# A third score bank in place of the maxima's start ring, one value product per slot, maxima spread between the scores, and the chunk loop written out

## The reference

```python
x = x + cross_attention(layernorm(x), ctx, ctx, tau, delta)      # 16 heads of 16, softmax over 1601
x = x + top1_expert_ffn(layernorm(x))                            # 8 experts, all computed, the chosen one kept
x = x + windowed_attention(ctx, layernorm(x), len, p_t)          # window of 256 keys, tanh
x = x + slot_ffn(layernorm(x))                                   # 64 slots, top-8 routing, slots gathered over all tokens
```

## Time and profile before

| | us |
|---|---|
| three timed runs, median | 1281.99 (1279.39 to 1282.0) |
| the profiled execution, its own time | 1280.34 |
| its span, first to last instruction | 1278.7 |
| PE busy | 1095.6 |
| VectorE (DVE) busy | 828.6 |
| ScalarE (ACT) busy | 549.9 |
| mean granted clock | 0.887 |

### The profile page before, as it was taken

The page is one execution under the profiler, slowest core; times in us unless marked ns, Lnnn a source line. Parts: engine busy times, 40 slices in busy tenths (PEclk is TensorE's granted clock), DMA queues, the critical chain, the costliest instruction groups (busy, mean ns, idle before and its releaser), DMA issues.

```text
span 1278.7 us, 20158 instructions
## 1 busy us (share of the span) xinstructions
PE 1095.6 (86%) x6460; PEld 438.7 (34%) x6460; DVE 828.6 (65%) x1814; ACT 549.9 (43%) x1020; POOL 44.2 (3%) x54
## 2 busy tenths in 40 slices
PE   6357999999999998898999989889999888977556
PEld 3232233333433333333333334323333243344324
DVE  4447988888776766676667765667667657644232
ACT  4121266666644444555444454555444436500220
POOL 3200000000000000000000000000000000010000
PEclk9876699999999987998999888989999889978765
DMA  8995000000000000001000000010000000100321
GB/s 240 144 114 184 1 8 7 14 14 2 30 14 1 13 1 1 14 2 48 2 13 1 14 1 13 1 49 1 14 1 14 1 14 1 46 1 0 109 75 66
DMA packets 44281, 41.19 MB, mean 32 GB/s; under 512 B 10109, under 2 KB 42334, under 8 KB 43914
## 3 DMA queue, kind: packets, MB, share of 16 engines
q1 hardware_dynamic: 41594, 38.17, 12.8%
q10 hardware_dynamic: 2496, 1.35, 0.7%
q0 software_dynamic: 80, 0.26, 0.2%
HBM read 29.52 MB, written 10.59 MB: 31 GB/s over the span
## 4 chain that ended last, share of the span: by engine, by line
PE 58%; DVE 16%; issue 13%; DMA 5%; SPq 4%; DVEq 2%; ACT 1%; POOL 0%; POOLq 0%; ACTq 0%
PE ps_o L748 17%; PE ps_m L672 15%; PE ps_e L903 11%; DVE mx L1055 10%; PE ps_m L779 7%; DMA k_stack<-q_stack 1%; DMA k_parts<-attn_chunk 1%; PE ps_m L969 1%; SPq L376 1%; PE ps_m L839 1%; PE ps_m L858 1%; PE ps_m L799 1%; SPq L352 1%; DMA q_stack<-mrow 1%; PE ps_m L860 1%
## 5 line engine op out<-in xcount | busy, mean ns | idle before, releaser
L1055 DVE TENSOR_REDUCE mx<-ps_m 128x1 f32<-128x401 f32 x1102 | 585.9, 570 | 259.6 <-PE ps_m L672 256.8
L564 ACT ACTIVATE probs<-ps_e 128x512 f32<-128x512 f32 (+1 forms) x832 | 457.7, 596 | 497.8 <-PE ps_e L903 496.5
L672 PE MATMUL ps_m<-k_stack,q_stack 99*128 99x401 bf16 x1102 | 401.5, 367 | 60.4 <-DVE mx L1055 51.7
L903 PE MATMUL ps_e<-q_stack,k_stack 101*128 101x512 bf16 (+1 forms) x832 | 337.3, 405 | 8.4 <-issue 7.0
L748 PE MATMUL ps_o<-probs,v_heads 128*32 128x256 f32 (+1 forms) x3328 | 280.3, 410 | 0.0
L672 PEld LDWEIGHTS ps_m<-k_stack,q_stack 99*128 99x128 bf16 x1102 | 109.4, 99 | 309.2 <-DVE mx L1055 266.5
L903 PEld LDWEIGHTS ps_e<-q_stack,k_stack 101*128 101x128 bf16 (+1 forms) x832 | 84.6, 102 | 152.8 <-ACT probs L564 64.8
L779 PE MATMUL ps_m<-expert_w,xnT 128*128 128x512 f32 x256 | 121.3, 605 | 6.3 <-DVE xb L1119 4.7
L748 PEld LDWEIGHTS ps_o<-probs,v_heads 128*32 128x32 f32 (+1 forms) x3328 | 67.1, 110 | 156.9 <-issue 132.5
L1119 DVE SCALAR_TENSOR_TENSOR xb<-ps_m,hot,xb 128x256 f32<-128x256 f32 x112 | 54.2, 484 | 17.9 <-PE ps_m L779 8.3
L779 PEld LDWEIGHTS ps_m<-expert_w,xnT 128*128 128x128 f32 x256 | 47.1, 194 | 47.9 <-issue 35.8
(11 more groups left out here) (213 smaller groups left out, 612.5 us busy)
## 6 DMA issues: line engine op xcount, KB each, us to landing
q_stack<-q_parts SPq DMA_DIRECT2D x114, 64.0 KB, 2.2
k_stack<-k_parts SPq DMA_DIRECT2D x18, 256.0 KB, 14.0
q_parts<-attn_chunk SPq DMA_DIRECT2D x6, 384.0 KB, 5.5
expert_w<-in_expert_wT SPq DMA_DIRECT2D x2, 1024.0 KB, 5.9
xres<-in_x SPq DMA_DIRECT2D x4, 512.0 KB, 3.5
x<-xres SPq DMA_DIRECT2D x4, 512.0 KB, 3.8
probs<-x SPq DMA_DIRECT2D x1, 2048.0 KB, 10.7
out<-probs SPq DMA_DIRECT2D x4, 512.0 KB, 2.9
```

The lines of the kernel that those rows point to most:

```text
L564: act.activation(probs[0:n, k % 2, h, :], ps_e[h % 2][0:n, :], ACT.Exp).then_inc(s["exp_done"], 1)
L672: pe.matmul(ps_m[:, u % 2 if banks == 2 else (UNITS * n1 + u) % banks, 0:SPLIT], qst[0:MAX_ROW, g, h, P * t:P * t + P], kst[0:MAX_ROW, HG ...
L903: pe.matmul(ps_e[h % 2][0:n, :], kst[0:ROWS, HG * g + h, P * st:P * st + n], qst[0:ROWS, g, h, :], start=True, stop=True).then_inc(s["qk_r ...
L1055: dve.tensor_reduce(mx[:, q, col:col + 1], ps_m[:, bank_of, 0:SPLIT], AX.X, ALU.max)\
```

## The change

- `ps_e` gets a third bank; a score waits for the exp three scores back instead of two.
- `ps_x` is no longer a bank of its own but the last bank of `ps_m`; turned maxima ("m") and turned `ps_o` ("o") become jobs that take their turn with the jobs of `behind` in two banks. Since they come at other places than once per chunk, jobs are numbered over all chunks.
- The ring of the maxima has two banks everywhere, at the start too.
- The value product is one per head and slot, over 512 tokens, at the slot's end.
- A unit follows each score; the fifth stands ahead of score 2, or, in a slot with an expert, a unit stands between the two halves of the expert's contraction and one behind each of the other scores. No unit follows the value product.
- VectorE takes unit 0 before its step of `behind` and does `max_columns` right behind the last unit of a group.
- The loops over chunks are Python loops, so offsets and waits are constants.

The rest of the diff is the new argument of `bank`, `filled` and `taken`, and constants in place of `bass.ds`.

```diff
+RING = 2
+EB = 3
...
-JOBS = (["ota", "otb", "y0", "y1", "t1a", "t1b", "router"] + [f"e{i}" for i in range(4)] + ["gateT"] + [f"e{i}" for i in range(4, 8)]
-        + ["gb0", "gb1"] + [f"e{i}" for i in range(8, 16)]
-        + ["t2a", "t2b", "score0", "score1", "aTa", "aTb", "z0", "z1", "t3a", "t3b", "h", "logits", "slots", "alphaT"])
-JOB = {name: i for i, name in enumerate(JOBS)}
-USES = len(JOBS) // 2
-assert len(JOBS) % 2 == 0
+BEHIND = {3: ["ota", "otb"], 5: ["y0"], 6: ["y1"], 9: ["t1a", "t1b"], 10: ["router"],
+          **{11 + i: [f"e{i}"] for i in range(8)}, 15: ["gateT", "e4"], 19: ["gb0", "gb1"],
+          **{20 + i: [f"e{8 + i}"] for i in range(8)}, 30: ["t2a", "t2b"], 31: ["score0", "score1"], 34: ["aTa", "aTb"],
+          35: ["z0"], 36: ["z1"], 39: ["t3a", "t3b"], 40: ["h"], 41: ["logits"], 44: ["slots", "alphaT"]}
...
+def has_expert(k):
+
+    return 11 <= k < 19 or 20 <= k < 28
...
+def job_numbers():
+
+    order = [("m", 0)]
+    for c in range(NC):
+        for k in range(SLOTS):
+            g, st = divmod(k, ST)
+            if c:
+                order += [(name, c - 1) for name in BEHIND.get(k - SHIFT, [])]
+            if st == 2 and (c or g):
+                order.append(("o", NG * c + g - 1))
+            if max_end(k - 1) is not None:
+                order.append(("m", NG * c + max_end(k - 1)))
+    order.append(("o", NG * NC - 1))
+    order += [(name, NC - 1) for k in range(SLOTS) for name in BEHIND.get(k, [])]
+    return {job: i for i, job in enumerate(order)}
+
+
+JOB = job_numbers()
...
-        ps_e = [ps(f"ps_e{i}", [P, CT]) for i in range(2)]
-        ps_m = ps("ps_m", [P, 4, CT])
+        ps_e = [ps(f"ps_e{i}", [P, CT]) for i in range(EB)]
+        ps_m = ps("ps_m", [P, RING + 2, CT])
         ps_o = ps("ps_o", [P, CT])
-        ps_x = ps("ps_x", [P, CT])
+        ps_x = ps_m[:, RING + 1, :]
...
-        def bank(job):
-            return ps_m[:, 2 + JOB[job] % 2, :]
+        def bank(job, c):
+            return ps_m[:, RING + JOB[job, c] % 2, :]
 
         def bank_free(eng, job, c):
 
-            need(eng, bank_taken[JOB[job] % 2], USES * c + JOB[job] // 2)
-
-        def filled(mm, job):
-            mm.then_inc(bank_filled[JOB[job] % 2], 1)
+            need(eng, bank_taken[JOB[job, c] % 2], JOB[job, c] // 2)
...
-                    act.activation(probs[0:n, k % 2, h, :], ps_e[h % 2][0:n, :], ACT.Exp).then_inc(s["exp_done"], 1)
+                    act.activation(probs[0:n, k % 2, h, :], ps_e[(HG * (SLOTS * c + k) + h) % EB][0:n, :], ACT.Exp).then_inc(s["exp_done"], 1)
...
             def take_o(c, g):
                 act.wait_ge(s["pv_done"], SLOTS * c + ST * (g + 1))
-                need(act, s["att_ready"], NG * c + g)
+                if NG * c + g:
+                    wait_filled(act, "o", NG * c + g - 1)
...
-            def max_unit(u, c, j, banks=2):
+            def max_unit(u, c, j):
 
 
                 g, n1 = j % NG, NG * c + j
                 t, h, q = u // (QUARTERS * HG), (u // QUARTERS) % HG, u % QUARTERS
                 if u == 0:
                     pe.wait_ge(q_loaded[j % NG], 96 * (c + j // NG + 1))
-                need(pe, s["max_taken"], UNITS * n1 + u + 1 - banks)
-                pe.matmul(ps_m[:, u % 2 if banks == 2 else (UNITS * n1 + u) % banks, 0:SPLIT], qst[0:MAX_ROW, g, h, P * t:P * t + P],
+                need(pe, s["max_taken"], UNITS * n1 + u + 1 - RING)
...
             def max_rows(n1):
 
-                need(pe, s["att_ready"], n1 - 1)
                 pe.wait_ge(s["mx_ready"], n1 + 1)
-                pe.transpose(ps_x[0:HG * TT, 0:P], mxc[:], ident[:]).then_inc(s["mT_ready"], 1)
+                bank_free(pe, "m", n1)
+                filled(pe.transpose(bank("m", n1)[0:HG * TT, 0:P], mxc[:], ident[:]), "m", n1)
...
-                max_unit(v % UNITS, 0, v // UNITS, banks=4)
+                max_unit(v % UNITS, 0, v // UNITS)
...
-            def pv(c, k, half):
-
-                cols = slice(CT // 2 * half, CT // 2 * (half + 1))
+            def pv(c, k):
+
                 g, st = k // ST % NG, k % ST
                 n = rows_of(st)
-                if half == 0:
-                    if st == 0:
-                        need(pe, s["o_taken"], NG * c + g)
-                    pe.wait_ge(s["exp_done"], HG * (SLOTS * c + k + 1))
+                if st == 0:
+                    need(pe, s["o_taken"], NG * c + g)
+                pe.wait_ge(s["exp_done"], HG * (SLOTS * c + k + 1))
                 for h in range(HG):
-                    mm = pe.matmul(ps_o[32 * h:32 * h + 32, cols], v_sb[0:n, st, HG * g + h, :],
-                                   probs[0:n, k % 2, h, cols], start=(st == 0 and half == 0),
-                                   stop=(st == ST - 1 and half == 1))
-                if half == 1:
-                    mm.then_inc(s["pv_done"], 1)
-
-            def turn_o(c, g):
-
-                pe.wait_ge(s["o_taken"], NG * c + g + 1)
-                pe.wait_ge(s["mrow_ready"], NG * c + g + 2)
+                    mm = pe.matmul(ps_o[32 * h:32 * h + 32, :], v_sb[0:n, st, HG * g + h, :], probs[0:n, k % 2, h, :],
+                                   start=(st == 0), stop=(st == ST - 1))
+                mm.then_inc(s["pv_done"], 1)
+
+            def turn_o(n):
+
+                pe.wait_ge(s["o_taken"], n + 1)
+                bank_free(pe, "o", n)
                 for t in range(TT):
-                    mm = pe.transpose(ps_x[:, P * t:P * t + P], o_raw[:, P * t:P * t + P], ident[:])
-                mm.then_inc(s["o_turned"], 1)
+                    mm = pe.transpose(bank("o", n)[:, P * t:P * t + P], o_raw[:, P * t:P * t + P], ident[:])
+                filled(mm, "o", n)
...
-            def experts(i, c):
+            def experts(i, c, units):
 
                 name, t, j = f"e{i}", i // 4, i % 4
                 bank_free(pe, name, c)
                 for k in range(KT):
-                    mm = pe.matmul(bank(name), xnT[:, k, P * t:P * t + P], expert_w[:, k, CT * j:CT * j + CT],
+                    if k:
+                        next_unit(units)
+                    mm = pe.matmul(bank(name, c), xnT[:, k, P * t:P * t + P], expert_w[:, k, CT * j:CT * j + CT],
                                    start=(k == 0), stop=(k == KT - 1))
-                filled(mm, name)
-
-            def behind(c, k):
+                filled(mm, name, c)
+
+            def next_unit(units):
+
+                for c, j, u in itertools.islice(units, 1):
+                    max_unit(u, c, j)
+
+            def behind(c, k, units=()):
...
-                    units = units_of(k)
+                    units = iter([(c, j, u) for j, u in units_of(k)])
+                    spare = len(units_of(k)) - HG
                     for h in range(HG):
                         if h == 2:
                             if not first:
-                                behind(c - 1, k - SHIFT)
-                            if k or not first:
-                                pv(c, k - 1, 0)
-                        need(pe, s["exp_done"], HG * SLOTS * c + HG * k + h - 1)
-                        pe.matmul(ps_e[h % 2][0:n, :], kst[0:ROWS, HG * g + h, P * st:P * st + n],
+                                behind(c - 1, k - SHIFT, units)
+                            if first or not has_expert(k - SHIFT):
+                                for _ in range(spare):
+                                    next_unit(units)
+                        need(pe, s["exp_done"], HG * SLOTS * c + HG * k + h + 1 - EB)
+                        pe.matmul(ps_e[(HG * (SLOTS * c + k) + h) % EB][0:n, :], kst[0:ROWS, HG * g + h, P * st:P * st + n],
                                   qst[0:ROWS, g, h, :], start=True, stop=True).then_inc(s["qk_ready"], 1)
-                        for j, u in units[h:h + 1]:
-                            max_unit(u, c, j)
+                        next_unit(units)
+                    assert next(units, None) is None
                     if k or not first:
-                        pv(c, k - 1, 1)
-                    for j, u in units[HG:]:
-                        max_unit(u, c, j)
+                        pv(c, k - 1)
                     if st == 2 and (g or not first):
-                        turn_o(c, g - 1)
+                        turn_o(NG * c + g - 1)
                     if max_end(k - 1) is not None:
                         max_rows(NG * c + max_end(k - 1))
 
             chunk(0, True)
-            with pe.Fori(1, NC) as c:
+            for c in range(1, NC):
                 chunk(c, False)
-            for half in range(2):
-                pv(NC, -1, half)
-            turn_o(NC, -1)
+            pv(NC, -1)
+            turn_o(NG * NC - 1)
...
-            def normalise(c, g):
-
-                dve.wait_ge(s["o_turned"], NG * c + g + 1)
-                turned = ps_x[:].rearrange("p (t j e) -> p t j e", t=TT, j=HG)
+            def normalise(n):
+
+                wait_filled(dve, "o", n)
```

(31 more changed lines are left out.)

138 lines of the change are left out of this document (70 added, 68 removed).

## The result

The change made the kernel slower: 1323.9 us (median of 4 runs, 1321.5 to 1325.2) against 1280.7 beside it on the same chip, a ratio of 1.034 (95% interval 1.032 to 1.036). The forecast was 1296. The profiled execution took 1321.5 us, its span 1319.8. One run in this whole document, of the kernel `mix2` in part 6, was of a second, slower state (1418 us at a granted clock of 0.68) and is left out of its median. In the new kernel the score is L935, the maximum unit L699, VectorE's read of it L1083, the value product L773, the expert L804.

What follows compares the result with a forecast made beforehand. It took the attention loop to set the time, with PE busy over 90% in the passes. 1280.3 + 13.2 + 8.5 + 8.4 - 15 gave 1295.4, against the median about 1296 us; range 1272 to 1316.

Steps and rivals of the forecast that it cites:

- Plain slots: Attention slots without other work: 3.31 to 3.49 us, from waits for the two-bank ring; pass 0 +13.2 us.
- start: Maxima before pass 0, with two instead of four banks: +8.4 us.
- expert slots: Slots with an expert in the later passes: nothing waits, 4.55 us, -0.48 each.
- the loop's way back: Chunk loops written out save PE's issue time and the slow clock after it: 7.5 us, twice, -15 us.
- The three later passes: Passes that also carry the previous chunk's other work: +2.85 us each, +8.5 us for three.
- long-step slots: Eleven VectorE-bound slots per later pass, where the whole value product is exposed after VectorE's step: +6.4 us a pass.
- the walk: Slot timing stepped through from profiled operation times; gave 3.31 of 3.32 us measured for the old plain slot, 3.49 for the new.
- Job banks: Turned maxima and `ps_o` share two banks with other jobs in later passes; the next expert waits: +2.1 us per pass.
- Rival 1: PE never waits for the ring; plain slots in pass 0 below 3.31 us; about 1200 us; chance 0.10.
- Rival 2: Reading unit 0 first frees PE, so the 6.4 and 2.1 per pass vanish; 1271 to 1283 us; chance 0.15.
- Rival 3: The clock falls to 1.2 GHz in one plain slot in five; 1342 us; chance 0.07.
- Rival 4: Written-out code stalls as the loop did; 1311 us; chance 0.06.

Runs made afterwards that it cites:

- mix2: `mix` with value product halves in fewer slots of the later passes (0 to 3, 5 and 47 to 51), none with a job beside it; 1233.1 us.
- the change with PE kept busy: The change with score 2 repeated in PE's waits for VectorE's long steps in the three later passes, 258 more matmuls; 1285.6 us.
- written-out before: The kernel before with its chunk loops written out as Python loops, nothing else changed; 1266.7 us, ratio 0.988.
- written-out before so kept: The kernel before with loops written out, plus score 2 repeated in the waits of its long steps in the three later passes; 1248.8 us.
- step in front: The change with VectorE's step of the earlier chunk put back ahead of the slot's first maximum; 1271.7 us, ratio 0.991 to before.
- u_both: Kernel before, loops written out, with one value product at slot's end, fifth maximum behind it, and VectorE's first maximum ahead of its step; 1294.4 us.
- mix: The change with VectorE's step first, value product in halves in pass 0 and 18 slots of each later pass, three start banks; 1242.1 us.

## Why the prediction was right and wrong

- **Slower, by these parts: right** (forecast in brackets). Plain slots 3.52 us (3.49), pass 0 +13.2 (+13.2), start +9.0 (+8.4), expert slots 4.60 (4.55), the loop's way back 16 (15), third bank nothing in the total (0). The exact match of pass 0 is partly luck: its slot 1 alone takes 3.5 to 4.8 us in the profiles, with the clock.
- **The three later passes: wrong, +8.5 forecast, about +33 measured** (both without the loops' gain). The step that failed is the +6.4 a pass for the long-step slots, and within it that the time at 1.2 GHz was taken over from the rows of before, in the two longest steps alone. The mechanism was right and its size off. At full clock the term was sound: these slots take 62.9 us a pass in the change with PE kept busy (mean of 63.3, 62.7 and 62.6) and 57.0 in written-out before so kept: +5.9. With the clock as granted they take 74.8, 72.1 and 70.9 against 61.3, 60.6 and 59.7: +12.
- **In sums.** The change is 57.2 us over written-out before (1323.9 - 1266.7); forecast for that were 13.2 + 8.5 + 8.4 = 30.1. At kept clock it is 36.8 (1285.6 - 1248.8), so 6.7 us of the miss are terms of the walk (expert slots gained 0.43 us instead of 0.48, and slots 16, 20 and 21, in pass 3 +0.3, +0.5 and +0.15, were not in it). The other 20.4 (38.3 - 17.9) are the clock. Each of these differences of two totals is good to about 5 us.
- **The range.** Its upper bounds (+9, +17, +22, -7) add up to 1321 on 1280.3, and to 1323 on the median; I wrote 1315 and then 1316. The measured 1323.9 is beyond either.
- **What the walk did not look at.** I walked VectorE's step as 0.40 us later because one read precedes it, and against the old kernel that is what happened (+1.09 instead of +0.69). But it starts 1.49 us later than it could, because the read must itself wait for the value product. Comparing with the old kernel alone, I saw neither the hole of 0.91 us on VectorE nor that the change with the other order would be a gain.
- **Job banks: size right, place incomplete.** Slots 12 and 25 cost +2.2, +1.9 and +3.2 us a pass with PE kept busy (forecast +2.1; in the third pass slot 25 lost 1.7 to the clock all the same). Slot 20 was not in the sum: 5.70 instead of 5.23, the gate product waits 0.35 for the last expert's bank, which VectorE gives back behind the first maximum.
- **Rivals.** Rival 1 fell with the plain slot. Rival 2's number is nearly met with the step in front (1271.7; it gave 1271 to 1283), but its condition was put the wrong way round: reading the first maximum first is what costs. Rival 3 named the clock, but in plain slots; pass 0 held 0.99 with a wait of 0.28 after unit 1 in each slot, and of the 24 falls in passes 1 to 3 of the change 22 came in or behind waits of 1.2 to 4.0 us. The other two came in slot 20 of pass 2, behind a wait of 0.71, and in slot 11 of pass 1, the slot of the router's short products, with no wait above 0.6 before it; what made the clock fall there stays open. Rival 4 fell: no gap of that kind at the passes' borders.

On the price of a low clock: the Trainium skill (TensorE: Matmul & The Clock Gate, section "HAM oscillation — how this bites in real kernels") takes half of the throttled time as what it costs. From the windows, twice the missing clock times the length, passes 1 to 3 of the change had about 130 us at 1.2 GHz, and some 15 with PE kept busy; by the rule 57 us should come back, and the passes lost 34.8 (806.6 - 771.8). The trace does not agree: less came back than the rule gives. That PE waited for VectorE in part of that time would explain it; this was not tested apart, and a repeat that outlasts its wait would also take something away.

What stays open: the repeats were sized from the waits of one profile for each order, so the clock's part is a measured difference of two kernels and not a pure price; and why `u_both` shows so little interaction of order and product (5 us, not told from 0), where the new kernel has 52 us for the order, is argued from the step's start (+1.18 there against +0.69 with the product alone), not tested.

## What to carry to other kernels

When a long operation is put in one piece on the bounding engine, look at the hole it leaves on the engine that serves the ring, and put that engine's longest other work into the hole: the same line order was worth 9 us in the old kernel, 17 in the new one with a small hole and 52 with the whole hole. Price a longer wait at both clocks: here the long-step slots lost 5.9 us a pass at full clock and 12 at the clock as granted. If such a wait can't be removed, repeating a harmless matmul in it was worth 18 to 38 us here.

## What the hardware showed that I had not expected

- Extra matmuls made a kernel faster: 258 repeated scores, 60.6 us of additional PE busy time, took 38.3 us off the total.
- Edits don't add when they meet in one wait: in the new kernel putting the step in front took 52.2 us off, putting the fifth maximum last 26.2, and both together 43.2.
- A split value product costs in its own slot and in the next. In `mix` slots 36 and 41, with two halves, took 0.32 and 0.27 us more than with one product in the step-first kernel (6.84 against 6.52 in slot 36). Slots 7, 32 and 37 kept one product and took 0.22 more (5.02 against 4.80 in slot 7): the slot ahead of them now has its last maximum behind the product, and their second maximum waits for that one's bank.
